# An adaLN attention and MoE layer: the attention gate folded into the output weight, two more PSUM banks and doubled buffers for the first tiles, and a new order of steps

## The reference

```python
mod = (_silu(L0_c) @ L0_wmod).reshape(L0_c.shape[0], 6, 1, -1)
ga = (2 * (ga >= 0) - 1) * jnp.maximum(jnp.abs(ga), 0.25)
h = _layernorm(x, axis=-1) * (1 + ca) + sa
x = x + ga * _L0_attn_ref(h, ...)
h = _layernorm(x, axis=-1) * (1 + cb) + sb
x = x + gb * _L0_ffn_ref(h, ...)
```

## Time and profile before

| | |
|---|---|
| three runs | 1216.95, 1218.11, 1219.6 us; median 1218.11 |
| the profiled execution | 1219.15 us, span 1217.4 us |
| TensorE busy | 1161.7 us, 95% |
| VectorE busy | 975.9 us, 80% |
| ScalarE busy | 760.7 us, 62% |
| GpSimd busy | 493.7 us, 41% |
| mean granted TensorE clock | 0.988 |

### The profile page before, as it was taken

How to read it: one execution, slowest core, us unless ns; L and a number is a source line. 1 busy time by engine, 2 the same in 40 slices (tenths; PEclk the granted TensorE clock), 3 DMA queues, 4 the chain that set the end, 5 groups by cost and what they waited for, 6 DMA issues and landing times.

```text
span 1217.4 us, 25541 instructions
## 1 busy us (share of the span) xinstructions
PE 1161.7 (95%) x8905; PEld 877.7 (72%) x8905; DVE 975.9 (80%) x1881; ACT 760.7 (62%) x1507; POOL 493.7 (41%) x375
## 2 busy tenths in 40 slices
PE   8988999999999989999998999999999999999996
PEld 4455666555565555565557899999999999999983
DVE  4677787766657889786677889999999999999977
ACT  3456555556665535546754477777777777777741
POOL 1122222111122111111010248888878788778741
PEclk9999999999999989999999999999999999999999
DMA  9480000000000000004003279999999999999988
GB/s 348 152 333 1 1 10 10 10 10 2 15 10 10 10 1 23 1 10 115 23 21 124 84 212 297 302 298 302 295 300 296 298 295 297 301 300 294 299 238 294
DMA packets 75167, 189.95 MB, mean 156 GB/s; under 512 B 11544, under 2 KB 12184, under 8 KB 74832
## 3 DMA queue, kind: packets, MB, share of 16 engines
q1 hardware_dynamic: 44704, 116.27, 28.2%
q0 software_dynamic: 28672, 71.32, 23.7%
q10 hardware_dynamic: 1712, 1.32, 0.3%
HBM read 136.36 MB, written 52.51 MB: 155 GB/s over the span
## 4 chain that ended last, share of the span: by engine, by line
PE 71%; DVE 13%; DVEq 4%; issue 4%; ACT 4%; DMA 2%; POOL 1%; POOLq 0%; SPq 0%; ACTq 0%
PE ps L1349 22%; PE ps L1388 12%; PE ps L1168 8%; PE ps L1335 5%; PE ps L1153 4%; PE ps L1198 4%; PE ps L1113 4%; PE ps L1081 3%; DVE nmax L1631 2%; PE ps L1138 2%; DMA acc_dram<-y,slots 1%; DVEq L1705 1%; PE ps L1216 1%; PE ps L1185 1%; PE ps L1053 1%
## 5 line engine op out<-in xcount | busy, mean ns | idle before, releaser
L751 POOL DMA_INDIRECT acc_dram<-y,slots x128 | 249.6, 1950 | 78.1 <-issue 50.7
L1631 DVE TENSOR_REDUCE nmax<-ps 128x1 f32<-128x512 f32 (+3 forms) x304 | 190.8, 656 | 80.3 <-PE ps L1117 43.0
L860 ACT ACTIVATE probs<-ps 128x512 f32<-128x512 f32 (+1 forms) x320 | 159.0, 555 | 85.5 <-PE ps L1153 82.4
L702 POOL TENSOR_SCALAR_AFFINE_SELECT probs<-probs 128x512 f32<-128x512 f32 x64 | 43.1, 675 | 351.6 <-ACT probs L860 351.6
L736 POOL DMA_INDIRECT xg<-h_dram,slots x128 | 130.4, 1019 | 84.5 <-DVE slots L1822 40.5
L1113 PE MATMUL ps<-kpad,qpT 128*128 128x512 f32 (+3 forms) x384 | 144.5, 444 | 9.9 <-DVE nmax L1631 7.9
L1349 PE MATMUL ps<-x_hi,e_gu_hi 128*112 128x256 f32 (+1 forms) x768 | 120.1, 278 | 0.0
L1349 PE MATMUL ps<-x_hi,e_gu_lo 128*112 128x256 f32 (+1 forms) x768 | 119.6, 278 | 0.0
L1153 PE MATMUL ps<-qT,kT 98*128 98x512 f32 (+1 forms) x320 | 111.8, 428 | 2.6 <-ACT probs L860 1.9
L1349 PEld LDWEIGHTS ps<-x_hi,e_gu_hi 128*112 128x112 f32 (+1 forms) x768 | 105.7, 179 | 5.9
L1349 PE MATMUL ps<-x_lo,e_gu_hi 128*112 128x256 f32 (+1 forms) x768 | 109.9, 279 | 0.0
(11 more groups left out here) (238 smaller groups left out, 2409.1 us busy)
## 6 DMA issues: line engine op xcount, KB each, us to landing
e_gu<-in_gate_up SPq DMA_DIRECT2D x64, 704.0 KB, 7.4
e_d<-in_w_down SPq DMA_DIRECT2D x64, 224.0 KB, 4.7
acc_dram<-h SPq DMA_DIRECT2D x2, 4608.0 KB, 25.8
e_d<-in_w_down SPq DMA_DIRECT2D x64, 128.0 KB, 5.4
wmod_b<-in_wmod SPq DMA_DIRECT2D x2, 2048.0 KB, 23.6
xg<-h_dram SPq DMA_DIRECT2D x16, 256.0 KB, 6.6
acc_a<-acc_dram SPq DMA_DIRECT2D x8, 512.0 KB, 10.9
acc_b<-acc_dram SPq DMA_DIRECT2D x8, 512.0 KB, 6.6
```

Of the source, the lines that this page charges most:

```text
L751: pool.indirect_dma_start(out=acc_dram[a], out_offset=bass.IndirectOffsetOnAxis(ap=slots[:, at:at + 1], axis=0), in_=y[e % 2][:, h, :], in ...
L860: act.activation(probs[:, n % PROBS, 2 * pr:2 * pr + 2, off:CW], unit_bank(2 * n + pr)[:, :, off:CW], ACT.Exp).then_inc(s_exp, 1)
L1631: dve.tensor_reduce(nmax[:, 1 if lo else 0, first:first + heads], max_view(n, heads, hi - lo), AX.X, ALU.max, negate=True).then_inc(s_max, 1)
```

## The change

The steps of a tile stay what they are. What differs:

1. scale_out multiplies the output weight by w_pre and by the gate row ga of a batch, once per batch (slots 24 to 27 and 201 to 204). For batch 1 the unscaled weight is loaded anew, when tile 7 has been projected. The first projection of each batch waits for it on TensorE. The residual is one instruction.
2. xn, hT and qk have two halves, used by even and odd tiles. turn_x of tiles 1 to 4 writes bank 1, pack and pack_keys of tiles 0 to 2 write bank 0, both before scores use them. The waits of these steps are changed to fit.
3. The shift and scale rows are made by two ScalarE instructions at slot 10; the modulation matmuls move to slots 0 to 3, and the gate rows to slots 5 and 7.
4. Fillers, places and the order inside the slot are new on all four engines.
5. The scratch in SBUF for the descriptors of GpSimd's DMAs is 8192 bytes per partition, where the default is 16384; wpre moves out of an early area, and ve2, rstd2 and oms share a tile.

```diff
+        SCALE_AT = 24, 201
-        STEPS_OVER = [32, 32, 32, 32, 32, 32, 32, 32]
-        DIVIDED = [4, 4, 2, 4, 4, 4, 4, 2]
+        STEPS_OVER = [32, 33, 32, 32, 32, 32, 32, 32]
+        DIVIDED = [3, 3, 2, 4, 3, 4, 4, 4]
-        MOD_AT, ROWS_AT = (2, 3, 4, 5), (6, 7, 8)
+        MOD_AT, ROWS_AT = (0, 1, 2, 3), (5, 7, 10)
+        SHIFT_AT = 10
-        STATS_AT = 11, 4 * H + 3, 8 * H + 3
+        STATS_AT = 11, 4 * H + 6, 7 * H + 5
...
+        MOVED = {"normalise": (-3, 0, -3, 0, 0, -2, 0, 0, -3, 0, 0, 0, 2, 0, 0, 1),
+                 "turn_x": (-14, 3, -1, 2, 1, 0, 0, 0, 1, 0, 0, 0, 0, 0, 1, 0),
+                 "modulate": (-5, 1, 0, 3, 0, 0, 0, 0, 0, 0, 0, -1, 0, 0, 0, 0),
...
+                 "rotate": (1, 1, -3, 0, -1, 1, 0, 2, 0, -1, 0, 1, 0, 0, 1, 0),
+                 "head_rms": (1, -2, -3, -2, 0, 3, 0, -1, 0, 2, -2, 0, -1, 0, -1, 0),
...
+                 "pack": (0, 2, 0, 0, 0, 1, 1, 1, 0, -1, 0, 1, 0, 0, 0, 0),
+                 "pack_keys": (1, 2, 0, 2, 0, 0, 0, 1, 1, -1, 1, 1, 0, 2, 0, 0),
...
+        EARLY_PACKS, EARLY_TURNS = 3, 5
+        def pack_bank(t):
+            return S_BANK if t < EARLY_PACKS else T_BANK
+        def turn_bank(t):
+            return S_BANK + 1 if 1 <= t < EARLY_TURNS else T_BANK
...
             for t in range(CT * CLOSE):
+                if t == TPB:
+                    sp.wait_ge(s_at, TPB)
+                    sp.dma_start(wo[:, :, :], wo_t).then_inc(s_wo, 16)
...
+            def shift_rows():
+                src = ps[:, Z_BANK, :]
+                shift, scale = slice(LANE, LANE + B), slice(2 * LANE, 2 * LANE + B)
+                act.wait_ge(s_gate_rows, 1)
+                act.activation(mod_rows[shift, :], src[shift, :], ACT.Copy)
+                act.activation(mod_rows[scale, :], src[scale, :], ACT.Identity, bias=1.0).then_inc(s_rows, 1)
...
             def turn_x(t):
                 keep_warm(("turn_x", t))
                 pe.wait_ge(s_xn, t + 1)
-                if t:
+                if 1 <= t < EARLY_TURNS:
+                    pe.wait_ge(s_hT, t)
+                elif t:
                     pe.wait_ge(s_qk, t)
...
             def pack(t):
                 keep_warm(("pack", t))
                 pe.wait_ge(s_parts, t + 1)
-                pe.wait_ge(s_hT, min(t + 3, NT))
-                pe.wait_ge(s_qk, min(t + 2, NT))
-                if t >= 2:
+                if t < EARLY_PACKS:
+                    if t:
+                        pe.wait_ge(s_packT, t)
+                else:
+                    pe.wait_ge(s_hT, min(t + 3, NT))
+                    pe.wait_ge(s_qk, min(t + 2, NT))
                     pe.wait_ge(s_qT, (t - 1) * NG)
...
             def out_project(t, half):
                 q, j = divmod(t, CT)
+                if half == 0 and t % TPB == 0:
+                    pe.wait_ge(s_scaled, t // TPB + 1)
...
                 if n == 0:
-                    if t == 0:
-                        dve.wait_ge(s_gates, 32)
                     dve.wait_ge(s_orstd, q + 1)
                     dve.wait_ge(s_at, t + 1)
-                    dve.scalar_tensor_tensor(scratch[:, :], ps[:, tile_bank(t), :], orstd[:, q % 2, j:j + 1], ga[:, t // TPB, :],
-                                             ALU.mult, ALU.mult).then_inc(s_atd, 1)
-                    dve.drain()
-                    dve.tensor_tensor(xt, xt, scratch[:, :], ALU.add)
+                    dve.scalar_tensor_tensor(xt, ps[:, tile_bank(t), :], orstd[:, q % 2, j:j + 1], xt,
+                                             ALU.mult, ALU.add).then_inc(s_atd, 1)
...
-            def scale_out(cc):
+            def scale_out(b, cc):
                 if cc == 0:
-                    dve.wait_ge(s_late, 80)
-                dve.tensor_scalar(wo[:, cc, :], wo[:, cc, :], wpre[:, cc:cc + 1], None, ALU.mult)
+                    if b == 0:
+                        dve.wait_ge(s_late, 80)
+                        dve.wait_ge(s_gates, 32)
+                    else:
+                        dve.wait_ge(s_wo, 16)
+                last = dve.scalar_tensor_tensor(wo[:, cc, :], wo[:, cc, :], wpre[:, cc:cc + 1], ga[:, b, :],
+                                                ALU.mult, ALU.mult)
+                if cc == KC - 1:
+                    last.then_inc(s_scaled, 1)
...
-    nc = bacc.Bacc("TRN2", target_bir_lowering=False, num_devices=1)
+    nc = bacc.Bacc("TRN2", target_bir_lowering=False, num_devices=1, dynamic_dma_scratch_size=8192)
```

More of the change, by code:

```diff
@@ L474, in build_program @@
         AT = {"normalise": -42, "turn_x": -38, "modulate": -37, "project_kv": -28, "project_q": -26,
-              "key_value_out": -27, "query_out": -23, "squares": -22, "rotate": -14, "head_rms": -11, "split": -9,
+              "key_value_out": -27, "query_out": -23, "squares": -22, "rotate": -14, "head_rms": -10, "split": -9,
               "second_high": -8, "pack": -4, "pack_keys": -3, "pack_out": -4, "keys_out": -3, "end_max": 16,
[L477 to L492, removed]
-                 "keys_out": (0, 0, 0, 0, 0, 0, 0, 0, 0, 0, 1, 0, 0, 2, 0, 1),
-                 "end_max": (0, 0, 0, 0, 0, 0, 0, 0, 0, 0, 0, 0, 0, 0, 0, 1),}
@@ L714, in _ @@
                         tiles_rstd(k)
-                for tile, _ in tile_due(m, "rstd"):
-                    tile_rstd(tile)
+                for q in chunk_due(m, "row_rms"):
+                    row_rms(q)
+                for tile, _ in due(m, "head_rms"):
+                    head_rms(tile)
                 for q, g, kt in steps_at(m):
@@ L719, in _ @@
                         causal(q, g, kt)
-                for tile, _ in due(m, "head_rms"):
-                    head_rms(tile)
+                for tile, _ in tile_due(m, "rstd"):
+                    tile_rstd(tile)
             row_rms(CLOSE)
@@ L1293, in _ @@
                         values(q, g, kt // 2)
-                if m in MOD_AT:
-                    modulation_rows(MOD_AT.index(m))
+                for tile, _ in due(m, "pack"):
+                    pack(tile)
+                if m == H:
+                    pe.wait_ge(s_late, 80)
+                for q in chunk_due(m, "gram"):
+                    gram(q)
+                for tile in range(3 * RT):
+                    if m == place_at(tile):
+                        place(tile)
                 for tile, _ in due(m, "turn_x"):
@@ L1301, in _ @@
                     project_kv(tile, 2 * n + 1)
+                for tile, half in tile_due(m, "project", 2):
+                    out_project(tile, half)
+                for tile, _ in due(m, "pack_keys"):
+                    pack_keys(tile)
                 for tile, n in stack_due(m):
@@ L1895, in _ @@
                         end_statistics(k)
+                for tile, n in due(m, "rotate", 4):
+                    rotate(tile, n)
+                for r in range(NR - 1):
+                    for n in range(ROUTED):
+                        if m == route_at(r, n):
+                            route(r, n)
+                for q in chunk_due(m, "mean_square"):
+                    mean_square(q)
+                for tile, _ in tile_due(m, "shift"):
+                    shift(tile)
+                if m in ROWS_AT[0:2]:
+                    modulation_rows(ROWS_AT.index(m))
+                for tile, n in due(m, "split", 4):
+                    split(tile, n)
                 if m == (NT + 1) * H + 1:
                     shared_up_lo()
-                for tile, n in due(m, "split", 4):
-                    split(tile, n)
+                for tile, n in tile_due(m, "residual", 2):
+                    residual(tile, n)
+                for b in range(B):
+                    if m == (NT + 1) * H + 11 + 3 * b:
+                        shared_gated(b)
+                    if m == (NT + 1) * H + 13 + 3 * b:
+                        shared_down_lo(b)
             def rows_lo(n, p):
```

223 lines of the change are left out of this document (102 added, 121 removed).

## The result

**1207.42 us**, median of 5 runs (1207.07 to 1208.98), against 1218.81 (5 runs, 1216.95 to 1219.6): ratio 0.9917, 95% interval 0.9906 to 0.9928. The kernel became faster by 11.4 us between the medians; forecast were 4.3. The direction was right and the value lies in the range, but the size is 2.6 times the forecast.

What follows compares the result with a forecast made beforehand. Bounds: TensorE's own work in the middle, VectorE from 410 to 510 us, latency chains in fill and tail. Terms -0.8 +1.5 -1 -3 -1 = -4.3 gave 1214.85 us, 1213.8 against the median; range 1202 to 1223.

Steps and rivals of the forecast that it cites:

- Places and orders refitted: Steps moved by slots on all engines: -3 us from 110 to 410 us and -1 from 510 to 640.
- fill: Start of the kernel, a latency chain: -1.5 +1.1 +0.8 -1.7, taken as -1 us, bounds -4 and +2.
- the 1.7 for tile 2's rotation: In the fill: rotation moves from slot 18 to 15, so VectorE's 1.69 us wait for rr goes, -1.7 us.
- batch change: Second weight scaling at about 422 to 429 us, less two residuals: net +1.5 us, bounds -1.5 and +6.4.
- tail: Residuals of tiles 14 and 15 lose their separate add, the second saving mostly waited out: -0.8 us.
- The waits for nmax from 410 to 510: Sign on TensorE: 5 to 8 us if the forecast is right, above 8 for the slower rival.
- The second scaling on VectorE's path: Four weight-scaling instructions at about 422 to 429 us, ahead of the reductions, delay VectorE by 3.0 us.
- The return of the residuals: One-instruction residuals give back 1.5 us on VectorE in the 410 to 510 us stage and 0.8 in the tail.
- The term of +0.8: In the fill: three of the first four weight scalings lie before tile 2's split is done, +0.8 us.
- The second scaling starves TensorE: Slower rival, 422 to 429 us: 3.0 us waiting plus 3.4 from a half-clock stretch, 1223.7 us; chance 0.22.
- The refit does much more: Rival: half the idle time from 110 to 640 us and half the 410 to 510 clock loss return, 1201.2; chance 0.14.
- The ring: Rival: with halved descriptor scratch GpSimd waits in every expert step, 0.5 us more on 62 steps, 1249 us; chance 0.02.

## Why the prediction was right in direction and wrong in size

- **The step that failed** is the term "Places and orders refitted": -3 for 110 to 410 and -1 for 510 to 640. Measured it is worth 6.6 to 8.2 us. Its bound (8.3 us won) came from a list of TensorE's waits from 110 us on, and the forecast was half of three of them. Two things in that were wrong. It gave the refit nothing in the fill, beyond the 1.7 for tile 2's rotation that stands in another term. There the runs show 3.9 us: the first Gram product begins at 135.83 us with the tables and orders of before and at 131.89 with the new ones, all else equal. With only the tables or only the orders of before it begins at 137.35 and 136.59 us. For the two stretches that it did price, the pieces give 2.1 + 1.5 = 3.6 of the 4.0 foretold. And it took waits for separate matters: neither tables nor orders bring anything alone, and GpSimd's order by itself decides over 7.5 us. Beside the forecast, with pieces that fit its stretches only roughly:

| piece | foretold | measured, all edits |
|---|---|---|
| fill | -1 | -4.2 |
| to the second Gram product | -3 | -4.6 |
| batch change | +1.5 | +0.9 |
| to the last one | -1 | -2.8 |
| tail | -0.8 | -1.0 |

- **The clock** I had counted as a second loss (7 us from 410 to 510) and priced only in a rival. It is a smaller part than the two profiles suggest: at most 8.4 of their 11.8 us, at most 3.4 of the 10.6 between all runs. 450 to 460 us went from 0.66 to 1.00, but the piece up to the second Gram product won 4.6 us at a clock of 1.00 before and after.
- **The signs.** The idle sum from 110 to 410 came as forecast (near 10.6; 11.0 measured). The waits for nmax from 410 to 510 were to be 5 to 8 us and were 2.5. The first transposes of the tail were to come 0.8 us earlier after the Gram product and came 0.6 earlier (12.13 us behind it before, 11.52 after). The average wait from 110 to 410, called under 0.5 us, is 8.3 us in 16, or 0.52.
- **In-order queues** appear in the prediction as a reason for losses ("in-order queues bring others"). The runs showed that GpSimd's order, worth nothing in the kernel before, is worth 7.5 us in the changed one. For head_rms I had written down the swap, and looked only at what the masks lose by it.
- **Fold.** The second scaling on VectorE's path: 3.0 foretold, 2.2 measured at the end, 3.1 at tile 12. The return of the residuals, 2.3 foretold (1.5 + 0.8), is 2.2 + 1.2 = 3.4 by two differences, the smaller of which is open. Net +0.7 foretold, about -1.2 measured. The new instruction's size was right:

```profile
L1858 DVE SCALAR_TENSOR_TENSOR wo<-wo,wpre,mods x8: 737/744/1167, 66.0 to 425.6; 128x512 f32<-128x512 f32 x8
```

- **The reload** was free, as foretold: issued at 400.5 us, landing 5.3 us later, ahead of the scaling at 415.17:

```profile
wo<-in_wo_t SPq DMA_DIRECT2D x1, 1024.0 KB, 5.3
```

- **The fill.** Foretold -1, measured -0.8 at the first row maximum of tile 2 (75.28 to 74.48). The wait for rr is gone:

```profile
65.38 0.72 DVE L1638 TENSOR_TENSOR t<-t,rr 128x544 f32<-128x544 f32 x1
```

  But the last part of that split begins at 70.63, where 71.43 was the earlier trace rows: 2.3 us earlier at the start of the split, 0.8 at its end. Three scalings of 0.74 us lie inside it now, where two of 0.48 lay, and 0.2 us of waiting. The term of +0.8 (3 x 0.27) took the three for lying there before as well; it should have been 3 x 0.75 - 2 x 0.48 = 1.3. Up to the Gram product the fill gained 4.2, half of it past 94 us, and 3.2 in TensorE's busy time; that part I had not seen.
- **The tail.** Foretold -0.8 for tiles 14 and 15; the last piece is 1.0 shorter. One instruction stands where two stood:

```profile
633.09 0.75 DVE L1696 SCALAR_TENSOR_TENSOR xres<-ps,orstd,xres 128x512 f32<-128x512 f32 x1 [0.16 <-issue]
633.93 0.69 DVE L1699 BATCH_NORM_STATS2 st<-xres 128x6 f32<-128x512 f32 x1
```

- **The rivals.** "The second scaling starves TensorE" had its mechanism half right: the stretch is 0.9 us longer, with waits of 1.74 and 1.35 and a clock of 0.83 from 420 to 430 (0.87 before). But its condition, nmax waits above 8 us, did not come (2.5). "The refit does much more" (0.14) took half of the idle time and half of the clock's loss, 16.9 us. Its 1201.2 missed by 6.2 us, my 1213.8 by 6.4, so neither is the better number. Its clock half, 3.5, is about what all runs show at most (3.4); its idle half, 13.4, was wrong (1.8 by the pieces). The ring is out: 7.37 us a step.

What stays open: what the 4.0 us of busy time are that TensorE saved without a higher clock; how the refit's worth splits between waits and clock, since each removed wait can change both; what the new early fillers and ScalarE's order are worth alone; and which of the moved steps matter, for the tables were tried only as a whole. Where a half-clock stretch falls differs between executions: from 90 to 100 us the profile of the changed kernel reads 1.00 and that of the kernel without the second scaling, whose code is the same up to there, 0.83. So 1 to 2 us between single profiles prove nothing.

## What to carry to other kernels

In a kernel whose order is written by hand, places and orders on the queues are one edit: try them together, and look on every in-order queue for a long instruction behind a short one whose input is not there yet. Compare two kernels over stretches of the same work and split each into busy and idle time of the bounding engine. Before less busy time is called the clock, compare it with the clock column of the piece and with the mean clock of all runs: here a single profile made the clock's part look more than twice as large as the runs allow. A list of waits in one stage prices neither the other stages nor how the steps act on each other. Remove fillers group by group now and then: a higher granted clock is no gain if the time doesn't fall.

## What was not expected of the hardware

- With 29 fillers the granted clock between 410 and 510 us is 0.98 in place of 0.95, and the kernel is about 3 us slower, while 44 others, where the clock would fall to 0.80 from 40 to 110 us, save 7.6.
- An operation with two full tensors on VectorE (128x512, f32) took 0.75 us, but 1.17 once, at 415.17 us. A GpSimd mask had begun at 415.15. The three parts of the split that took 1.14 us instead of 0.72 (at 84.38, 353.08 and 381.61 us) also begin within 0.1 us behind the start of a mask, as at 353.00 above. No run tests whether the mask is the cause.
- GpSimd's power of 128x17 elements takes 3.07 us, against 0.64 for a mask over 128x512. In GpSimd's queue its place ahead of a mask or behind one went with 7.5 us in the changed kernel and with nothing in the kernel before.
